# Row maxima of an attention kernel spread by a diagonal and a matmul of ones instead of two DMAs, with another order of jobs

## The reference, cut to what matters

```python
xn = layernorm(x)                                  # x: (1, 2048, 256), f32
k, q, v = W_K xn, W_Q xn, W_V xn                   # 16 heads of 128
scores = q k^T, causal mask
attn = softmax(scores / sqrt(128))
s = W_O (attn v)
g = silu(xn W_base^T + b_base + 2 * lora(xn))      # top-1 of 8 experts, rank 16
return x + s * g
```

## Time and profile before

| | |
|---|---|
| median of 3 runs | 1547.8 us (1547.08 to 1548.89) |
| profiled execution, own time | 1548.1 us |
| its span, first to last instruction | 1546.2 us |
| busy of the span: PE, DVE, ACT, POOL | 94%, 81%, 82%, 51% |
| mean granted TensorE clock | 0.989 |
| DMA, mean | 22 GB/s |

### The profile page before, as it was taken

The page is one execution under the profiler, slowest core; times in us unless marked ns, Lnnn a source line. Parts: engine busy times, 40 slices in busy tenths (PEclk is TensorE's granted clock), DMA queues, the critical chain, the costliest instruction groups (busy, mean ns, idle before and its releaser), DMA issues.

```text
span 1546.2 us, 23204 instructions
## 1 busy us (share of the span) xinstructions
PE 1459.5 (94%) x7788; PEld 1193.2 (77%) x7788; DVE 1248.1 (81%) x2541; ACT 1274.0 (82%) x2196; POOL 793.4 (51%) x688
## 2 busy tenths in 40 slices
PE   5999999999999999999999999999999999999997
PEld 4877778777877878777787777877787777877765
DVE  6788877888788886888868887788878898788864
ACT  2788898889888898898988888888987988888962
POOL 2444655455465555456554555554645555544740
PEclk9899999999999999999999999999999999999998
DMA  2100010000100001000010001000010000100002
GB/s 75 49 8 14 15 25 25 15 15 8 29 21 15 15 7 42 15 14 13 10 42 15 7 15 28 22 15 14 8 35 21 15 7 13 40 8 15 15 28 82
DMA packets 30070, 33.75 MB, mean 22 GB/s; under 512 B 11008, under 2 KB 17664, under 8 KB 29952
## 3 DMA queue, kind: packets, MB, share of 16 engines
q1 hardware_dynamic: 29952, 32.26, 8.3%
HBM read 30.02 MB, written 2.23 MB: 21 GB/s over the span
## 4 chain that ended last, share of the span: by engine, by line
PE 51%; ACT 24%; DVE 13%; issue 9%; POOL 2%; DMA 0%; SPq 0%; ACTq 0%; POOLq 0%; DVEq 0%
PE ps L281 15%; PE ps L282 14%; PE ps L283 14%; ACT ps L478 7%; ACT probs L498 7%; ACT p_hi L499 6%; DVE p_lo L551 6%; PE ps L719 4%; DVE partmax L566 3%; POOL colsum L433 2%; PE ps L754 2%; ACT qT_hi L486 1%; DVE z_lo L588 1%; ACT z_hi L504 1%; PE ps L731 1%
## 5 line engine op out<-in xcount | busy, mean ns | idle before, releaser
L433 POOL TENSOR_TENSOR colsum<-colsum,probs 128x512 f32<-128x512 f32 (+3 forms) x512 | 610.2, 1192 | 388.3 <-ACT probs L498 373.6
L478 ACT ACTIVATE ps<-maxrow 128x512 f32<-128x512 f32 (+3 forms) x640 | 645.3, 1008 | 8.9 <-DMA maxrow<-max_dram 8.7
L551 DVE TENSOR_TENSOR p_lo<-probs,p_hi 128x512 fp32r<-128x512 f32 (+3 forms) x640 | 614.9, 968 | 42.4 <-ACT p_hi L499 41.4
L498 ACT ACTIVATE probs<-ps 128x512 f32<-128x512 f32 (+3 forms) x640 | 362.9, 567 | 141.4 <-PE ps L731 74.8
L499 ACT ACTIVATE p_hi<-ps 128x512 fp32r<-128x512 f32 (+3 forms) x640 | 365.3, 571 | 0.0
L566 DVE TENSOR_REDUCE partmax<-ps 128x1 f32<-128x512 f32 x384 | 256.9, 679 | 10.4 <-PE ps L719 9.5
L281 PE MATMUL ps<-qT_hi,kT_hi 128*128 128x512 f32 (+3 forms) x640 | 247.6, 387 | 12.7 <-ACT ps L478 9.6
L281 PE MATMUL ps<-p_hi,v_hi 128*128 128x512 f32 (+3 forms) x640 | 241.7, 378 | 13.2 <-DVE p_lo L551 12.2
L282 PE MATMUL ps<-qT_lo,kT_hi 128*128 128x512 f32 (+3 forms) x640 | 234.3, 366 | 0.0
L283 PE MATMUL ps<-qT_hi,kT_lo 128*128 128x512 f32 (+3 forms) x640 | 233.9, 366 | 0.0
L282 PE MATMUL ps<-p_lo,v_hi 128*128 128x512 f32 (+3 forms) x640 | 233.5, 365 | 0.0
(11 more groups left out here) (106 smaller groups left out, 2174.8 us busy)
## 6 DMA issues: line engine op xcount, KB each, us to landing
maxrow<-max_dram SPq DMA_DIRECT2D x64, 256.0 KB, 3.8
wraw<-wqk_dram SPq DMA_DIRECT2D x16, 256.0 KB, 3.8
acc<-x_dram SPq DMA_DIRECT2D x4, 512.0 KB, 7.2
wraw<-wv_dram SPq DMA_DIRECT2D x8, 256.0 KB, 4.7
wraw<-wo_dram SPq DMA_DIRECT2D x8, 256.0 KB, 2.9
probs<-x_dram SPq DMA_DIRECT2D x4, 512.0 KB, 4.5
out_dram<-acc SPq DMA_DIRECT2D x4, 512.0 KB, 3.0
max_dram<-rowmax SPq DMA_DIRECT2D x64, 2.0 KB, 1.4
```

Of the source, the lines that this page charges most:

```text
L433: nc.gpsimd.tensor_tensor(total[:, c0:], total[:, c0:], tile[:, c0:], ALU.add)\
L478: nc.scalar.activation(st[job.n % SCORE_BANKS].rearrange("p (t n) -> p t n", t=TB)[:, q:, :], maxrow[:, job.g, :].rearrange("p (n t) -> p ...
L498: nc.scalar.activation(probs[:, k, c0:], src, ACT.Exp, scale=SCALE).then_inc(probs_ready, 1)
L551: nc.vector.tensor_tensor(p_lo[:, k, c0:], probs[:, k, c0:], f32(p_hi[:, k, c0:]), ALU.subtract)\
```

## The change

The two DMAs and their DRAM row go. In their place stands a job `Spread` per block:

- POOL multiplies the identity by the block's maxima: `diag[p, t, n]` = `rowmax[p, t]` if p = n, else 0; 128x512, fp32r, two buffers.
- PE multiplies a 128x128 matrix of ones by `diag` into an auxiliary bank: every partition then holds the sum over p, which is the maximum of query 128 t + n, in query order.
- ACT copies that with scale -1 to `maxrow`; DVE waits for the copy, and a memset of one column frees the bank.
- The seed reads `maxrow` straight, without rearrangement and with no scale.

POOL's part stands where the block's last `RowMax` job stands in the list; `with_spreads` puts the `Spread` job itself ahead of the third score tile after that (`SPREAD_LAG = 2`), and for the first two blocks ahead of the first score tile. The table `SCHEDULE` is another one, with the same kinds and numbers of jobs.

```diff
+SPREAD_LAG = 2
+Spread = namedtuple("Spread", "aux head g")
...
+def with_spreads(kinds):
+    out, due, tile = [], [], 0
+    for kind, args in kinds:
+        if kind is Score:
+            if tile == 0:
+                tile = SPREAD_LAG
+            tile += 1
+            while due and due[0][0] < tile:
+                out.append((Spread, due.pop(0)[1]))
+        out.append((kind, args))
+        if kind is RowMax and args[-1]:
+            due.append((tile + SPREAD_LAG, args[:2]))
+    return out
...
-    "V00 w Pq03 V01 w w z7 | | Pk02 | s7 Pk03 v V11 | o70 v M0222 | M0212 o71 v M0202 M0232 v | V21 S0 Z0 | v V10 "
+    "Pq03 w V01 Pk02 w w z7 V00 | | V21 | s7 M0212 v | M0311 M0222 o70 v | v o71 M0202 M0232 v | Z0 V10 | Pk03 "
...
-    return number(mark_last(kinds))
+    return number(with_spreads(mark_last(kinds)))
...
+        diag = sb("diag", [P, 2, TB, P], F32R)
...
# SP
-                if isinstance(job, RowMax) and job.last:
-                    blocks += 1
-                    row = max_dram[job.head * NB + job.g]
-                    sp.wait_ge(max_ready, blocks)
-                    sp.dma_start(row.rearrange("(p t) -> p t", t=TB), rowmax[:, job.g, :]).then_inc(max_out, 16)
-                    sp.wait_ge(max_out, 16 * blocks)
-                    if job.head:
-                        sp.wait_ge(seeded, tiles_until((job.head - 1) * NB + job.g))
-                    sp.dma_start(maxrow[:, job.g, :], row.partition_broadcast(P)).then_inc(max_spread[job.g], 16)
# POOL
+            def make_diagonal(job, block):
+                pool.wait_ge(max_ready, block + 1)
+                if block >= 2:
+                    pool.wait_ge(max_spread, block - 1)
+                nc.gpsimd.tensor_tensor(
+                    diag[:, block % 2, :, :], ident[:, None, :].broadcast_to([P, TB, P]),
+                    rowmax[:, job.g, :][:, :, None].broadcast_to([P, TB, P]), ALU.mult).then_inc(diagonal_ready, 1)
...
+                if isinstance(job, RowMax) and job.last:
+                    make_diagonal(job, blocks)
+                    blocks += 1
# ACT, the seed and the new copy
                 if job.kt == 0:
-                    act.wait_ge(max_spread[job.g], 16 * (job.head + 1))
-                q = columns(job) // P
-                nc.scalar.activation(st[job.n % SCORE_BANKS].rearrange("p (t n) -> p t n", t=TB)[:, q:, :],
-                                     maxrow[:, job.g, :].rearrange("p (n t) -> p t n", t=TB)[:, q:, :],
-                                     ACT.Copy, scale=-1.0).then_inc(seeded, 1)
+                    act.wait_ge(max_spread, max_blocks.index(job.head * NB + job.g) + 1)
+                c0 = columns(job)
+                nc.scalar.activation(st[job.n % SCORE_BANKS][:, c0:], maxrow[:, job.g, c0:], ACT.Copy)\
+                  .then_inc(seeded, 1)
...
+                elif isinstance(job, Spread):
+                    act.wait_ge(aux_full, job.aux + 1)
+                    if job.head:
+                        act.wait_ge(seeded, tiles_until((job.head - 1) * NB + job.g))
+                    nc.scalar.activation(maxrow[:, job.g, :], aux[job.aux % AUX_BANKS], ACT.Copy, scale=-1.0)\
+                      .then_inc(max_spread, 1)
# DVE
+                elif isinstance(job, Spread):
+                    dve.wait_ge(max_spread, max_blocks.index(job.head * NB + job.g) + 1)
+                    nc.vector.memset(wait_slot[:, job.aux % AUX_BANKS:job.aux % AUX_BANKS + 1], 0.0)\
+                      .then_inc(aux_free, 1)
# PE
+                elif isinstance(job, Spread):
+                    block = max_blocks.index(job.head * NB + job.g)
+                    pe.wait_ge(diagonal_ready, block + 1)
+                    nc.tensor.matmul(dst, ones_r[:, :], diag[:, block % 2, :, :].rearrange("p t n -> p (t n)"),
+                                     start=True, stop=True).then_inc(aux_full, 1)
```

More of the change, by code:

```diff
@@ L60, in number @@
             ev += 1
-        elif kind in (RowMax, Sums, Out):
+        elif kind in (RowMax, Sums, Out, Spread):
             plan.append(kind(aux, *args))
@@ L222, in attention_layer @@
         aux = [ps[:, SCORE_BANKS + 2 + k, :] for k in range(AUX_BANKS)]
-        max_dram = nc.dram_tensor("max_dram", (H * NB, BW), F32, kind="Internal").ap()
         x_in = [sem(f"x_in{b}") for b in range(NB)]
@@ L240, in attention_layer @@
         max_ready = sem("max_ready")
-        max_out = sem("max_out")
-        max_spread = [sem(f"max_spread{g}") for g in range(NB)]
+        diagonal_ready = sem("diagonal_ready")
+        max_spread = sem("max_spread")
         bits_set = sem("bits_set")
@@ L269, in attention_layer @@
         scores = [job for job in plan if isinstance(job, Score)]
+        max_blocks = [job.head * NB + job.g for job in plan if isinstance(job, Spread)]
         def columns(t):
@@ L333, in ffn_weights @@
                 sp.dma_start(wraw[:, 2, D:2 * D], bias.partition_broadcast(P)).then_inc(ffn_in, 16)
-            blocks = 0
             for job in plan:
-                if isinstance(job, RowMax) and job.last:
-                    blocks += 1
-                    row = max_dram[job.head * NB + job.g]
-                    sp.wait_ge(max_ready, blocks)
-                    sp.dma_start(row.rearrange("(p t) -> p t", t=TB), rowmax[:, job.g, :]).then_inc(max_out, 16)
-                    sp.wait_ge(max_out, 16 * blocks)
-                    if job.head:
-                        sp.wait_ge(seeded, tiles_until((job.head - 1) * NB + job.g))
-                    sp.dma_start(maxrow[:, job.g, :], row.partition_broadcast(P)).then_inc(max_spread[job.g], 16)
                 if not isinstance(job, Score):
@@ L415, in _ @@
             nc.gpsimd.memset(acc[:, :, :], 0.0).then_inc(acc_clear, 1)
-            his = 2
+            his, blocks = 2, 0
             for job in plan:
+                if isinstance(job, RowMax) and job.last:
+                    make_diagonal(job, blocks)
+                    blocks += 1
                 if not isinstance(job, Score):
```

## The result

The changed kernel takes 1460.98 us (median of 4 runs, 1459.41 to 1462.19) against 1547.76 us: ratio 0.944, 95% interval 0.942 to 0.945.

A forecast was written before the change was run, and what follows sets the result against it. No engine is full: four engines in fixed order hold each other up, ACT waited for most because of strided seeds. Span 1546.2 + 15 + 2 - 56 = 1507, as median 1508.5 us; range 1478 to 1530 (0.69).

The forecast's parts named there:

- Point 2: On PE: 64 added matmuls of 512 columns at 0.235 us, paid in full, +15 us.
- Point 3: On POOL: 64 diagonals, 66 us (upper bound 98), hidden if ready when PE comes; cost 0, at most below 10 us.
- Rival E: PE waits for POOL's diagonal, so the kernel is slower though the seed is fast; 1567 us at 0.9 us each; chance 0.05.
- Point 6: Waits given back across the engines: for seeds, for p_lo and p_hi, and for auxiliary banks; sum -56 us.
- (c): Auxiliary banks: DVE's waits for v_hi and p_hi shrink by 35 us, offset by 32 of new waits; net 6 us back.
- point 4: On DVE: 64 memsets, 4 us, each waiting 0.5 us for ACT's copy, 32 us of DVE's idle time.
- (a): PE's waits for seeds, 46.5 us, and the slower restart behind each of the 106: 38 us back.
- (b): Waits for p_lo and p_hi: ACT is earlier and DVE follows; half of 24.7, 12 us back.
- Point 7: The two removed DMAs and the new order of jobs: nothing taken, the order's effect left to the range.
- Rival B: DVE takes ACT's place, slowed by POOL's added work on shared SBUF interfaces; 1532 us, range 1530 to 1545; chance 0.11.
- D: The seed keeps its time because SBUF as source, not the stride, costs 1.0 ns a column; 1572 us; chance 0.07.
- C: Nearly all waits for ACT go and the order uses it; 1475 us, range 1462 to 1478; chance 0.08.

The follow-up runs named there:

- dma_copy_old: The kernel before, with both DMAs and the old order, plus one ACT copy per block into query order so that seeds read contiguously: 1472.69 us.
- dma_pool_old: The kernel before, with both DMAs and the old order, plus one POOL copy per block into query order so that seeds read contiguously: 1461.02 us.
- mm_cont_old: The changed kernel with the old table of jobs; diagonal, matmul of ones and contiguous seeds stay: 1480.31 us.
- mm_lag0: The changed kernel with SPREAD_LAG 0 in place of 2, the matmul of ones two tiles earlier: 1714.55 us.
- mm_str_new: The changed kernel with the row in maxrow in the old layout, so that seeds read every fourth float; matmul and new order stay: 1593.92 us.
- dma_str_new: The kernel before with the new table of jobs alone; DMAs and strided seeds stay: 1561.05 us.
- mm_str_old: The changed kernel with the row in the old layout (strided seeds) and the old table of jobs: 1584.58 us.

## Why the prediction was right in kind and wrong in size

- **Which engine is late and why** (the seed at every fourth float): right, and shown by the pairs that differ in the step alone, 133 and 104 us. The seed fell to 618 ns, inside the 600 to 660 named; ACT's busy time in the stretch is 1,038 us, forecast 1,003. From one start to the next the seed takes 0.52 us (910.44 to 910.96), 0.48 taken.
- **Point 2, +15 us on PE for 64 matmuls**: the size fits. The median distance from the start of a matmul of ones to the next start is 0.239 us, 15.3 us for 64. No run isolates what they add to the time: dma_copy_old and dma_pool_old, which have the order and contiguous seeds of mm_cont_old and no such matmul, are 8 and 19 us faster, but differ from it in other parts too.
- **Point 3, the diagonal hidden**: right, 1.2 us of waits once; 1281 ns of mean length against 1035 taken, inside the bounds. mm_lag0 shows what the cover is worth: 254 us, of which 158.5 are waits. Rival E's mechanism exists, at a lag that this kernel doesn't have.
- **Point 5, the start, +2 us**: 2.9.
- **Point 6, -56 us of waits, is the step that failed**, in its size and not in its sign, and within it part (c) with point 4. By the same count as before, 1,320 us of work in 1,358 leave some 40 us of standing and restarting where there were 140. The spans differ by 87.7 us; add the 15 of matmuls and the 2.9 of the start, and some 106 us came back. 19 of these need the new order (next point but one), so some 86 stand against the 56. The parts: (a) of 46.5 us for seeds 42 came back, forecast 38; (b) of 24.7 for `p_lo` 21, forecast 12; (c) of the waits for auxiliary banks 6 were to go, and practically all went, 32.6 and 22.6 us for the row maximum alone. (c) was a difference. DVE's waits for `v_hi` and `p_hi` were to shrink by 35 us, and they did by 30, from 105.4 to 75.7. Against that stood the 32 us of point 4, DVE waiting 0.5 us for each of ACT's 64 copies. That wait came twice and cost 0.9 us in all: the term set against the gain didn't exist. So the prediction, which had seen ACT behind DVE's waits, let next to nothing of PE's waits for banks go for it; mm_str_new shows that PE waits for `p_lo` and for row maxima when only ACT is slower. DVE's busy time fell by 60 us besides, which the sum didn't have, but that fall alone gave nothing: mm_str_new has it too. The rows count only part of what came back: behind a wait the next matmul restarts late, which the waits don't list.
- **The cross-check by the chain** (108 us of seeds cut to 58 us of gain) agreed with the wrong sum and made it look safe. It supposes that the rest of the chain stays; yet with PE at 95% of it after, exponentials, `p_hi` and `p_lo` left the chain with the seeds. That the seeds had put them there is shown by mm_str_new, where only the step is back and the chain is

```profile
PE 50%; ACT 28%; issue 12%; DVE 7%; POOL 2%; DMA 1%; SPq 0%; ACTq 0%; POOLq 0%; DVEq 0%
```

- **Point 7, nothing for the order**: the second term that was off, put at nothing without a row. As an edit by itself it is +12 us, with the change's other parts -19 us. Without the new order the kernel takes 1480 us, in the range; with it 1461.
- **Rival B** fell: DVE is 83% busy and PE hardly waits for it (3.5 us for `p_lo`); `p_lo` became shorter, not longer. **D** fell by the seed's length. **C**, given 0.08 at 1462 to 1478, named what happened, nearly all of ACT's waits gone and an order that uses them, and the time lies 1 us below it. It deserved more than 0.08: ACT was to fall from 87% of the stretch to 69%, and DVE as the next was at 82%. After, ACT is at 76% of a shorter stretch and DVE at 83%.

## What to carry to other kernels

An operand that is read 640 times and written 64 should be laid out for the reader: the step of four floats cost 0.54 us per read and 104 to 133 us in all, and each of three ways of reordering it once per block (a matmul, a copy on ACT, a copy on POOL) removed 76 us or more in at least one order. In a pipeline of engines with fixed order and few buffers, the waits shown against one engine may be another's, passed on. Here, where the engine waited for most got well clear, nearly all of PE's waiting went, and not only the rows that name it: a forecast should give such a case a real chance, and set a new wait against the gain only with a row that shows it. And an order of jobs belongs to the latencies it was made for: measured under other parts it can cost as much as it gives.

## What the runs showed of the hardware that I had not expected

- `p_lo` (DVE, two SBUF operands, 512 columns) fell from 1141 to 966 ns while POOL's share of the stretch rose from 54 to 64%. Each part of the change has a share, and they don't add up evenly: from the kernel before, the new order alone gives 1034 ns (dma_str_new), the matmul in place of the DMAs alone 1077 (mm_str_old); contiguous seeds take 84 ns off in the old order (1077 to 993) and 30 in the new (996 to 966). Why is open; when POOL runs beside it wasn't separated.
- A DMA of 2 KB in 512 single elements takes 8.2 us where the same bytes in runs of 16 take 1.4.
- PE's clock stood at its half, 1.2 GHz, from 37 to 47 us before; after the change matmuls still start 0.43 us apart at 50.50 and the granted clock over 47.2 to 58.0 is 0.81:

```profile
47.20:58.00 10.80, 10.04 (x56) 8.55 (x57) 3.30 (x6) 7.35 (x15) 1.01 (x2) 0.81 0.00 0
```

  With the later start the slow stretch is longer: 0.19 of 10.8 us is 2 us, of the 5 allowed for.
